# Two of the four picks of twelve token tiles gathered and added by GpSimd before the closing block of a routed layer

## What is computed

```python
scores = sigmoid(xf @ gate_w.T) + expert_bias          # 16 experts in 4 groups
# the 2 best groups, in them the 4 best experts; w: their scores, made to sum to 1
h = silu(einsum('td,edh->teh', xf, w1)) * einsum('td,edh->teh', xf, w3)
y = einsum('teh,ehd,te->td', h, w2, cw)                 # cw: w at the 4 picked experts, else 0
z = silu(xf @ sw1) * (xf @ sw3) @ sw2                   # two shared experts
x = layernorm(x + y + z)
```

## Time and profile before

| | us |
|---|---|
| median of 3 runs | 2362.14 (2360.26 to 2365.52) |
| the profiled execution | 2360.64 |
| its span in the profile | 2358.8 |
| attention, router and `front` | 0 to 1705 |
| `routed` | 1705 to 2246.9 |
| `combine` | 2246.9 to 2358.8 |

### The profile page before, as it was taken

How to read it: one execution, slowest core, us unless ns; L and a number is a source line. 1 busy time by engine, 2 the same in 40 slices (tenths; PEclk the granted TensorE clock), 3 DMA queues, 4 the chain that set the end, 5 groups by cost and what they waited for, 6 DMA issues and landing times. The chain is left out here.

```text
span 2358.8 us, 44567 instructions
## 1 busy us (share of the span) xinstructions
PE 2201.6 (93%) x13153; PEld 1968.2 (83%) x13154; DVE 1350.9 (57%) x4636; ACT 1132.9 (48%) x3690; POOL 1451.2 (62%) x2027
## 2 busy tenths in 40 slices
PE   6899999999999999999999999899999999988963
PEld 4789999899899899899899989467799999978852
DVE  5677677577577677677577678483222222222266
ACT  2556666566566566566566666541133332322221
POOL 2777666667567667566567666466471212799576
PEclk8999999999999999999999999999999999999986
DMA  5500510000000000000000000234362333555466
GB/s 144 201 22 21 230 61 22 3 21 21 3 21 19 5 22 19 5 22 19 5 21 19 4 1 1 66 104 165 116 188 95 111 105 114 165 184 183 127 174 183
DMA packets 68596, 177.75 MB, mean 75 GB/s; under 512 B 11584, under 2 KB 15232, under 8 KB 68224
## 3 DMA queue, kind: packets, MB, share of 16 engines
q1 hardware_dynamic: 36608, 84.93, 11.1%
q0 software_dynamic: 19504, 69.23, 9.6%
q10 hardware_dynamic: 12240, 20.73, 2.4%
HBM read 107.74 MB, written 67.13 MB: 74 GB/s over the span
## 5 line engine op out<-in xcount | busy, mean ns | idle before, releaser
L771 POOL TENSOR_TENSOR cross<-nat,rope_tables 128x128 f32<-128x128 f32 x256 | 150.3, 587 | 431.0 <-DVE nat L633 431.0
L926 PE MATMUL bank<-whi,xT_lo 128*128 128x384 f32 x1024 | 370.2, 362 | 3.1 <-PEq L177 2.0
L927 PE MATMUL bank<-wlo,xT_hi 128*128 128x384 f32 x1024 | 347.8, 340 | 0.0
L928 PE MATMUL bank<-whi,xT_hi 128*128 128x384 f32 x1024 | 347.7, 340 | 0.0
L592 DVE TENSOR_TENSOR acc<-acc,bank 128x512 f32<-128x512 f32 x256 | 175.9, 687 | 229.5 <-PE bank L928 213.4
L705 ACT COPY probT<-bank 128x128 f32<-128x128 f32 (+3 forms) x256 | 109.4, 427 | 385.2 <-PE bank L542 385.1
L926 PE MATMUL bank<-ring_hi,xslo 128*128 128x352 f32 x600 | 202.9, 338 | 18.3 <-issue 16.9
L1597 DVE TENSOR_TENSOR shlo<-bank,shhi 128x256 fp32r<-128x256 f32 x76 | 32.3, 424 | 296.4 <-ACT shhi L1565 296.4
L714 ACT ACTIVATE prob<-prob,nbias,rstd 128x256 f32<-128x256 f32 (+1 forms) x256 | 152.5, 596 | 103.0 <-DVE nbias L620 93.4
L926 PEld LDWEIGHTS bank<-whi,xT_lo 128*128 128x128 f32 x1024 | 196.0, 191 | 3.8 <-issue 2.3
L927 PEld LDWEIGHTS bank<-wlo,xT_hi 128*128 128x128 f32 x1024 | 196.3, 192 | 0.0
(11 more groups left out here) (271 smaller groups left out, 6189.7 us busy)
## 6 DMA issues: line engine op xcount, KB each, us to landing
staged<-in_wexp POOLq DMA_DIRECT2D x64, 544.0 KB, 4.2
slots_in<-zeros SPq DMA_DIRECT2D x41, 512.0 KB, 6.0
xslot<-slots_in SPq DMA_DIRECT2D x76, 256.0 KB, 2.7
slots_out<-yslot ACTq DMA_DIRECT2D x76, 256.0 KB, 2.0
wraw<-in_wh SPq DMA_DIRECT2D x16, 768.0 KB, 4.3
staged<-in_wexp SPq DMA_DIRECT2D x16, 544.0 KB, 3.7
slots_out<-zeros SPq DMA_DIRECT2D x9, 512.0 KB, 6.3
acc<-in_x SPq DMA_DIRECT2D x4, 1024.0 KB, 12.0
```

The source lines that it names most:

```text
L771: pool.tensor_tensor(cross[:, :, :], nat[:, a.two, :, 0:2 * ROT], sin, ALU.mult).then_inc(s_mult, 1)
L926: pe.matmul(out, wl_, xh_, start=first, stop=False)
L927: pe.matmul(out, wh_, xl_, start=False, stop=False)
L928: return pe.matmul(out, wh_, xh_, start=False, stop=last)
```

## The change

In `routed`, behind the last weight piece, GpSimd gathers picks 0 and 1 of tiles 0 to 11 in three batches of eight (`HELD`): batch 0 is pick 0 of tiles 0 to 7, batch 1 pick 0 of tiles 8 to 11 and pick 1 of tiles 0 to 3, batch 2 pick 1 of tiles 4 to 11. Their buffers are `staged` and slot 2 of the two rings. GpSimd multiplies each by its weight into `staged` and adds it to `acc`. Before batch 0 it waits for the stores of experts 0 to 12, before batch 1 for those of 0 to 14 (`stored_through`).

In `combine` the gathers are picks 2 and 3 of tiles 0 to 11 and all four of tiles 12 to 15, 40 instead of 64, in six sets of four buffers, with the power four tiles behind. The late chunk's blocks stand behind the sums of tiles 2, 4, 7, 10, 12 and 13; a block's down products come one block later, each block adding to all four results, and the split hidden units need two buffers instead of six. The late result is added to tiles 12 to 15 after all their sums, and their statistics follow there.

```diff
@@ routed, GpSimd @@
+                def stored_through(e):
+                    pool.wait_ge(y_out, first_of(pool, e + 1) * 16 + 16)
+                    pool.tensor_tensor(spare[:, 0:1], spare[:, 1:2], spare[:, 1:2], ALU.add)
+                def pick_ahead(j):
+                    for i in range(HELD):
+                        k, n = ahead(j, i)
+                        pool.indirect_dma_start(held(areas[j], i), None, ys[:, :],
+                                                bass.IndirectOffsetOnAxis(ap=slots[:, n, k:k + 1], axis=0),
+                                                bounds_check=MAXT * P - 1, oob_is_err=False).then_inc(s_ahead[j], 16)
+                def add_ahead(j):
+                    pool.wait_ge(s_ahead[j], 16 * HELD)
+                    wait_for(pool, s_added, j * HELD)
+                    for i in range(HELD):
+                        k, n = ahead(j, i)
+                        pool.tensor_scalar(held(staged, i), held(areas[j], i), pick_w[:, n, k:k + 1], 1.0,
+                                           ALU.mult, ALU.mult).then_inc(s_scaled, 1)
+                    pool.wait_ge(s_scaled, (j + 1) * HELD)
+                    for i in range(HELD):
+                        _, n = ahead(j, i)
+                        pool.tensor_tensor(acc[:, n, :], acc[:, n, :], held(staged, i),
+                                           ALU.add).then_inc(s_added, 1)
+                pool.wait_ge(s_w, QUARTERS * (LAST + 1))
+                stored_through(E - 4)
+                pick_ahead(0)
+                add_ahead(0)
+                stored_through(E - 2)
+                pick_ahead(1)
+                pool.wait_ge(s_ahead[1], 16 * HELD)
+                pick_ahead(2)
+                add_ahead(1)
+                add_ahead(2)
                 end = first_of(pool, E)
                 pool.wait_ge(y_out, end * 16 + 16)
...
@@ combine @@
-        NG = 4
-        LAG = 3
+        NG = 6
+        LAG = 4
+        BLOCK_AFTER = (2, 4, 7, 10, 12, 13)
+        def picks(n):
+            return range(2 if n < LATE else 0, PICK)
...
@@ combine, TensorE @@
                     mm.then_inc(s_up, 1)
-                pe.wait_ge(s_hlo, NB)
-                for i in range(TPC):
-                    cols = slice(i * P, (i + 1) * P)
-                    for q in range(NB):
...
+                    if q:
+                        down(q - 1)
+                down(NB - 1)
...
@@ combine, ScalarE @@
                     act.wait_ge(s_hid, q + 1)
+                    wait_for(act, s_ld, q - 1)
...
@@ combine, VectorE @@
+                for n in range(NT):
+                    sums(n)
+                    if n in BLOCK_AFTER:
+                        late_block(BLOCK_AFTER.index(n))
+                    if n < LATE:
+                        dve.wait_ge(s_sum, summed(n + 1))
+                        moments(n)
+                        if n:
+                            less_mean(n - 1)
+                dve.wait_ge(s_sum, summed(NT))
+                for n in range(LATE, NT):
+                    dve.wait_ge(s_y, n - LATE + 1)
+                    dve.tensor_tensor(acc[:, n, :], acc[:, n, :], b_y[n - LATE][:, :], ALU.add).then_inc(s_late, 1)
+                    dve.wait_ge(s_late, n - LATE + 1)
+                    moments(n)
+                    less_mean(n - 1)
                 less_mean(NT - 1)
```

More of the change, by code:

```diff
@@ L47 @@
 EARLY = NCH - 1
+HELD = 8
 RING = 4
@@ L1418, in _, with held, routed @@
                 add_shared(EARLY - 1)
-def routed(nc, t, bank, ident, xs, ys, tile_expert, first_tile, x, x_in, whi, wlo, staged, s_piece, sb, sem):
+def held(area, j):
+    return area[:, j * HID:(j + 1) * HID]
+def routed(nc, t, bank, acc, ident, xs, ys, slots, pick_w, tile_expert, first_tile, x, x_in, whi, wlo, staged, s_piece,
+           sb, sem):
     st = ExitStack()
@@ L1442, in routed @@
         y_out = sem("yslot_out", st)
+        s_ahead = [sem(f"picks_ahead{j}", st) for j in range(3)]
+        s_scaled, s_added = sem("picks_scaled", st), sem("picks_added", st)
         s_hi, s_w, s_xt, s_u1, s_u3, s_ht, s_dn, s_xhi, s_silu, s_hhi, s_y, s_xlo, s_h, s_hlo = (
@@ L1447, in routed, with ahead @@
         LAST = E + NSH - 1
+        areas = (staged, *(w[:, (E - 2) % RING, :].bitcast(F32) for w in (whi, wlo)))
+        def ahead(j, i):
+            return divmod(j * HELD + i, EARLY * TPC)
         def first_of(eng, e):
@@ L1620, in combine, with summed, landed, buffer @@
     with st:
[L1621 to L1622 removed]
+        NG = 6
+        LAG = 4
         NB = NSH * HB
         LATE = EARLY * TPC
[L1625 to L1627 removed]
+        BLOCK_AFTER = (2, 4, 7, 10, 12, 13)
+        areas = (staged, *(w[:, (E - 2) % RING, :].bitcast(F32) for w in (whi, wlo)))
+        got = [held(areas[j // HELD], j % HELD) for j in range(NG * PICK)]
+        spare_hi, spare_lo = (w[:, (E - 1) % RING, :] for w in (whi, wlo))
         xhi, xlo = (spare_hi[:, j * KC * CH:(j + 1) * KC * CH].rearrange("p (k c) -> p k c", k=KC) for j in range(2))
[L1629 removed]
+        hhi, hlo = (spare_lo[:, j * 2 * CH:(j + 1) * 2 * CH].rearrange("p (b c) -> p b c", b=2) for j in range(2))
+        def picks(n):
+            return range(2 if n < LATE else 0, PICK)
+        def summed(n):
+            return sum(len(picks(m)) for m in range(n))
+        def landed(n):
+            return 16 * sum(len(picks(m)) for m in range(n % NG, n + 1, NG))
+        def buffer(n, k):
+            return got[n % NG * PICK + k]
         gate = [sb(f"late_gate{i}", [P, CH], F32, st) for i in range(2)]
@@ L1653, in _, with down @@
                 pe.wait_ge(s_xlo, KC)
+                def down(q):
+                    s, b = divmod(q, HB)
+                    rows = hb_rows(b)
+                    lo_, hi_ = w2_cols(b)
+                    pe.wait_ge(s_hlo, q + 1)
+                    for i in range(TPC):
+                        cols = slice(i * P, (i + 1) * P)
+                        mm = three_products(pe, b_y[i][:, :], (hhi[0:rows, q % 2, cols], hlo[0:rows, q % 2, cols]),
+                                            (whi[0:rows, slot(s), lo_:hi_], wlo[0:rows, slot(s), lo_:hi_]),
+                                            q == 0, q == NB - 1)
+                        if q == NB - 1:
+                            mm.then_inc(s_y, 1)
+                    if q < NB - 1:
+                        mm.then_inc(s_ld, 1)
                 for q in range(NB):
@@ L1706, in gather @@
                     if n >= NG:
-                        pool.wait_ge(s_sum, PICK * (n - NG + 1))
-                    for k in range(PICK):
-                        pool.indirect_dma_start(got[n % NG][:, k, :], None, ys[:, :],
+                        pool.wait_ge(s_sum, summed(n - NG + 1))
+                    for k in picks(n):
+                        pool.indirect_dma_start(buffer(n, k), None, ys[:, :],
                                                 bass.IndirectOffsetOnAxis(ap=slots[:, n, k:k + 1], axis=0),
@@ L1747, in _, with sums, moments @@
                                       ALU.subtract).then_inc(s_xlo, 1)
[L1748 to L1757, removed]
+                def sums(n):
+                    dve.wait_ge(s_got[n % NG], landed(n))
+                    for i, k in enumerate(picks(n)):
+                        if i:
+                            dve.wait_ge(s_sum, summed(n) + i)
+                        dve.scalar_tensor_tensor(acc[:, n, :], buffer(n, k), pick_w[:, n, k:k + 1],
                                                  acc[:, n, :], ALU.mult, ALU.add).then_inc(s_sum, 1)
-                    if 1 <= n <= NB:
-                        late_block(n - 1)
-                    dve.wait_ge(s_sum, PICK * (n + 1))
+                def moments(n):
                     dve.bn_stats(stats[:, n % 2, :], acc[:, n, :]).then_inc(s_st, 1)
```

22 lines of the change are left out of this document (7 added, 15 removed).

## The result

| | before | after |
|---|---|---|
| median | 2363.35 us of 4 runs (2360.26 to 2365.52) | 2401.39 us of 4 runs (2399.63 to 2403.92) |
| ratio | | 1.0163, 95% interval 1.015 to 1.0176 |
| profiled execution, its span | 2360.64, 2358.8 | 2403.92, 2402.1 |

The changed kernel is 38 us slower; the forecast was 2397 with a range of 2388 to 2408. Its profiled execution runs some 4.6 us later already ahead of the change: the last weight piece ends at 2221.01 + 2.54 = 2223.55 for 2218.9, and GpSimd's first step of the routed block starts at 1709.58 for 1705.07. The changed kernel of experiment 5 ends that piece at 2219.20, so this is a difference between executions and not the change's doing.

What follows compares the result with a forecast made beforehand. GpSimd's issue of gathers was taken to bound the close. 2218.9 + 86.6 (work ahead) + 1.3 (hand-over) + 87.0 (close) = 2393.8 us of span, plus 1.8 around it and 1.5 to the median: 2397 us, range 2388 to 2408.

Steps and rivals of the forecast that it cites:

- GpSimd's gathers bound the close: In the close, GpSimd's issue of gathers sets the pace: 6.05 us a tile, while VectorE needs less.
- The work ahead, 86.6 us: Behind the last weight piece, GpSimd's 24 gathers, 24 scalings and 24 additions with waits and small steps take 86.6 us.
- The row of the same instruction: For GpSimd's additions ahead: the profile row of L785, the identical instruction, taken as the size, 1.289 us each.
- The hand-over, 1.3 us: From GpSimd's end of the work ahead to the start of the close: 1.3 us, range 0.3 to 5.8.
- The rival at 0.17: At the routed block's end, the barrier's 5.8 us belong to GpSimd's own ending and follow its last addition: 2401.6; chance 0.17.
- The close, 87.0 us: From TensorE's first transpose to the span's end: 87.0 us, 24.9 less than before, with last statistics starting at 79.8.
- TensorE sets the end: In the close, late blocks at half clock make the last down products come late: 2401 to 2407 us; chance 0.16.
- hidden after all: Ahead of the close, the work ahead fits GpSimd's 28 us cover, making the kernel faster: 2337 us; chance 0.03.
- The sum: Whole kernel: last weight piece's end, work ahead, hand-over and close give a 2393.8 us span, and a forecast median of 2397.

Runs made afterwards that it cites:

- experiment 5: The changed kernel with the power three tiles behind the gathers in the close (`LAG = 3`) for four: 2398.03 us, ratio 1.0156.
- Experiments 2 and 3: First: kernel before with only the new close, all 64 gathers in it: 2370.13 us. Second: changed kernel with one batch of three ahead: 2367.48 us.
- 4: The changed kernel without the 24 scalings and 24 additions ahead, its gathers kept: 2361.83 us, ratio 0.9995.
- run 10: The kernel before and its close, with picks 0 and 1 of tiles 0 to 3 gathered ahead and a GpSimd drain behind them: 2346.70 us, ratio 0.9927.
- run 12: As run 10, with the powers up to tile 7 four tiles behind the gathers and not three: 2346.91 us, ratio 0.9927.
- runs 7 and 8: Kernel before, 12 gathers ahead, a drain in front, sums on VectorE: 2351.70 us; the second also spreads the late blocks over more tiles: 2352.66 us.
- experiments 3 to 12: Four variants of the changed kernel, then six of the kernel before with 12 or 8 gathers ahead: medians from 2346.70 to 2402.17 us.

## Why the prediction was right, point by point

- *GpSimd's gathers bound the close*: right. With 24 gathers gone the close fell from 111.9 to 85.65 us, and from 2330.78 to the gathers of tile 15 GpSimd never stood longer than 0.31 us. VectorE was held by the power less often than was said: of its eleven `less_mean` steps up to tile 10 five waited (4.10, 0.37, 3.01, 1.12 and 3.00 us).
- *The work ahead, 86.6 us*: 85.3. Additions 1.22 for 1.289 (-1.5 in all), scalings 0.67 for 0.70 (-0.6), gathers 1.31 for 1.37 (about -1.3), landings 2238.79 - 2234.37 = 4.42 and 2267.99 - 2263.63 = 4.36 for 3.66 (+1.5); the rest is small steps. The row of the same instruction was right to decide: the 48 instructions took 45.5 us, where twice VectorE's 0.785 would have made 37.7. The fault is in what was doubled and not in the Trainium skill's "about twice" (GPSIMD Engine Reference, Engine selection), which this trace bears out for the addition alone: 1.22 us on GpSimd, 0.69 for VectorE's addition of the same shape (L1852), 1.8 times. VectorE's 0.785 is a scaling and an addition in one instruction, for which GpSimd needs two.
- *The hand-over, 1.3 us*: **the step that was mis-sized.** It was 7.6. The prediction took the end of the block before, where VectorE ended last, as nearest. There too GpSimd has a drain of 5.3 us (64 scatters), but it begins at 1689.7, while VectorE still works, and is hidden:

```profile
L1038 POOLq DRAIN  x1: 5297/5297/5297, 1689.7 to 1689.7; - x1
```

  Here GpSimd ends last, so nothing hides its drain, and it grows by the 24 gathers that the change adds. The rival at 0.17, that the 5.8 us are GpSimd's own ending, was the right mechanism. That its 2401.6 came so near is in part luck: its 5.8 us were 1.8 short, and the work ahead and the close, which it shares with the forecast, 2.6 too long. The engines that wait were no reason for a short hand-over, and the trace of before held the row, at the block's own line.
- *The close, 87.0 us*: 85.65. Up to the last statistics it went as worked out, 80.3 for 79.8. From there to the end it took 5.3 for 7.2: the last drain now covers 40 DMAs and not 64 (3921 ns for 5887).
- *TensorE sets the end*, *hidden after all*: both false. VectorE had no wait for the late products at 2390.67, and the work ahead was 85 us, not 51.6.
- *The sum*: hand-over +6.3, work ahead -1.3, close -1.35 make 2400.6 from 2397; measured 2401.4. Experiments 2 and 3 came out within 1.2 us of the same arithmetic; in 4 it left out a wait and was 5.8 off.

## What to carry to other kernels

Work put into an engine's idle gap is free only up to the gap's length, and an operation that another engine does in one instruction and 0.785 us should not be bought there for 1.9. Eight gathers ahead instead of 24, the sums left on VectorE, the old close and a drain in the gap turned +1.6% into -0.7%, of which the drain alone is 0.25. At the end of a block look at the block's own line in the trace: GpSimd's drain there grew with the DMAs issued, every engine waited for it, and a drain put early into the same gap took it away. When the bound engine's gap is short, look first at what starts the next stage soonest: four gathers more ahead gained nothing here.

One such place is left untested. The kernel ends with the same drain, 5.3 us before the change, and GpSimd stands idle 4.64 and 4.40 us ahead of its last two powers; a drain there, behind the last gather, might hide most of it.

## What the runs showed of the hardware

- A GpSimd drain cost 0.083 us for each DMA that GpSimd had issued since the last one, though all had landed (24 to 88 DMAs, table above), and 0.06 us with none issued since.
- With gathers still in flight it took longer: 72 DMAs 7.0 us from the last gather's end in run 10 (2232.4 to 2239.4) and 6.4 in run 12, and 12 DMAs 3.6 and 3.2 in runs 7 and 8. It did not take the landing and the count's price one behind the other: in run 7 it ended 0.5 us behind the last landing, in run 10 3.0.
- A store of 256 KB issued behind three or more gathers of a row, while the row went on, landed in 3.8 to 4.2 us (the changed kernel and experiments 3 to 12), behind one in 2.1 to 3.1, and with none being issued in 2.0 to 2.2.
- GpSimd's addition of 128x512 took 1.22 us with the other engines idle against 1.289 in the attention part.
